# Four graph layers on one core: the expansions of the cell lists load the key rows of two groups with one transfer

## The reference, cut to what matters

```python
# layer 2: both directions of each edge
h = x @ W.T + b
msg = h[src] * norm
out = jax.ops.segment_sum(msg, dst, num_segments=num_nodes)
...
# layer 3: source rows alone are fetched
h_src = feat_n[src]
copy_sum = jax.ops.segment_sum(h_src, dst, num_segments=N)
...
# layer 4: both directions, attention with a softmax over the edges of a node
logits = jax.nn.leaky_relu(s_node[src] + d_node[dst] + e_all, NEG_SLOPE) / T
h_src = xt[src]
out = jax.ops.segment_sum(att[:, None] * h_src, dst, num_segments=num_nodes)
```

## Time and profile before

| what | value |
|---|---|
| device time, median of 3 runs | 18736.65 us (18729.88 to 18747.82) |
| profiled execution, span from first to last instruction | 18902.1 us |
| mean granted TensorE clock | 0.647 of full speed |
| busy over the span: PE, DVE, POOL, ACT | 60%, 54%, 48%, 24% |
| DMA issues of key rows by SP in the three expansions | 1632 of list 1, 1088 of list 0 |
| DMA issues of stores by SP in them | 1088 of 192 KB, 544 of 132 KB |

### The profile page before, as it was taken

The page is one execution under the profiler, slowest core; times in us unless marked ns, Lnnn a source line. Parts: engine busy times, 40 slices in busy tenths (PEclk is TensorE's granted clock), DMA queues, the critical chain, the costliest instruction groups (busy, mean ns, idle before and its releaser), DMA issues. The chain is left out here.

```text
span 18902.1 us, 333620 instructions
## 1 busy us (share of the span) xinstructions
PE 11316.2 (60%) x72558; PEld 8597.6 (45%) x72559; DVE 10279.5 (54%) x36111; ACT 4453.3 (24%) x11901; POOL 9045.6 (48%) x10035
## 2 busy tenths in 40 slices
PE   6555555555544666666586666655555665557886
PEld 5333333333333555555475444442223554336776
DVE  9555555555551333333564777773345554777776
ACT  0111111111110222222211342005400112555665
POOL 0555666555562555555674344540263344553332
PEclk9676677666665666666555566765555555557887
DMA  9522222222213222222433698766642777885454
GB/s 378 209 64 64 64 63 64 64 67 61 63 58 64 56 57 57 57 57 57 73 58 36 227 307 283 216 190 215 200 127 69 222 230 222 262 259 178 172 172 140
DMA packets 2144090, 2589.10 MB, mean 137 GB/s; under 512 B 892242, under 2 KB 1761563, under 8 KB 2143939
## 3 DMA queue, kind: packets, MB, share of 16 engines
q1 hardware_dynamic: 1748902, 1741.10, 31.4%
q0 software_dynamic: 353792, 654.90, 11.7%
q10 hardware_dynamic: 41244, 191.56, 2.6%
HBM read 1738.16 MB, written 848.30 MB: 137 GB/s over the span
## 5 line engine op out<-in xcount | busy, mean ns | idle before, releaser
L565 POOL DMA_INDIRECT edges_by_dst<-rec,pos x1568 | 1538.0, 981 | 2027.1 <-DVE rec L500 1577.6
L983 POOL DMA_INDIRECT sc_rows<-src_table,sc_idx x1664 | 1581.7, 951 | 1470.2 <-DVE sc_tp L1081 820.7
L565 POOL DMA_INDIRECT edges_by_cell<-rec,pos x1568 | 1549.2, 988 | 528.9 <-issue 527.4
L1719 PE MATMUL ex_rows<-table,ex_oh 128*128 x6528 | 1177.8, 349 | 830.4 <-DVE ex_oh L1687 406.7
L1805 PE MATMUL gs_part<-gs_rows,gs_oh 128*128 128x192 bf16 x6528 | 1093.2, 329 | 789.5 <-DVE gs_oh L1778 403.9
L1033 PE MATMUL sc_loc<-dst_table,sc_ohT 128*128 x3328 | 772.2, 405 | 1137.7 <-ACT sc_ohT L999 1090.8
L1767 POOL DMA_INDIRECT gs_rows<-rows_by_src,chunk_read_by_src x1088 | 1072.3, 986 | 759.5 <-PE gs_part L1805 441.2
L2213 PE MATMUL at_part<-cell_edge_term,key_in_block 128*66 128x128 f32 x8704 | 1229.6, 306 | 251.0 <-issue 211.5
L1719 PEld LDWEIGHTS ex_rows<-table,ex_oh 128*128 128x128 bf16 x6528 | 755.2, 132 | 1252.9 <-issue 1213.7
L2213 PEld LDWEIGHTS at_part<-cell_edge_term,key_in_block 128*66 128x66 f32 x8704 | 1143.0, 159 | 326.4 <-issue 314.8
L529 DVE SCALAR_TENSOR_TENSOR junk<-rowb,keycol,earlier 128x128 f32<-128x128 f32 (+1 forms) x3136 | 1150.7, 413 | 199.5 <-issue 195.3
(11 more groups left out here) (394 smaller groups left out, 25919.0 us busy)
## 6 DMA issues: line engine op xcount, KB each, us to landing
ex_keys<-src_key_rows SPq DMA_DIRECT2D x1632, 128.0 KB
rows_by_src<-ex_stage SPq DMA_DIRECT2D x1088, 192.0 KB
rowb<-sort_key_rows SPq DMA_DIRECT2D x392, 512.0 KB
ex_keys<-dst_key_rows SPq DMA_DIRECT2D x1088, 128.0 KB
dst_rows_by_src<-patY ACTq DMA_DIRECT2D x1, 104448.0 KB
gs_rows<-dst_rows_by_src SPq DMA_DIRECT2D x544, 192.0 KB
scored_dst_rows_by_src<-patZ ACTq DMA_DIRECT2D x1, 71808.0 KB
scored_rows_by_src<-ex_stage SPq DMA_DIRECT2D x544, 132.0 KB
```

Of the source, the lines that this page charges most:

```text
L565: nc.gpsimd.indirect_dma_start(out=out, out_offset=bass.IndirectOffsetOnAxis(ap=pos[:, u, k, j:j + 1], axis=0), in_=row, in_offset=None).t ...
L983: nc.gpsimd.indirect_dma_start(out=rows[:, u, j, :], out_offset=None, in_=tabS, in_offset=bass.IndirectOffsetOnAxis(ap=idx[:, u, j:j + 1], ...
L1719: m = nc.tensor.matmul(rows[k][u % 2][r // 2][:, r % 2, 0:W], oh[k][:, u % 2, r * P:(r + 1) * P], t3[:, bass.ds(held[k][u], 1), :].rearran ...
```

## The change

A load moves the keys of two groups, 2048 bytes into each partition, and is issued at even steps only. Its wait asks for one more group's one-hots than before, since it writes two slots. There is one key semaphore for each pair of slots. The bytes that are moved, the ring of four slots, and the work of all other engines are the same. The edit is the same in `expand_rows` and in `attention_rows`; one of them stands here.

```diff
-def row_of(kr, g):
+def row_of(kr, g, count=1):
 
     at = kr[0:1, 0:1]
-    return bass.AP(tensor=at.tensor, offset=at.offset + g * (SLOTS * P), ap=[[0, P], [1, SLOTS * P]])
+    return bass.AP(tensor=at.tensor, offset=at.offset + g * (SLOTS * P), ap=[[0, P], [1, count * SLOTS * P]])
...
-        s_key = {k: [counts.get(f"expand_keys_loaded{k}{u}") for u in range(RING)] for k, _, _ in lists}
+        s_key = {k: [counts.get(f"expand_keys_loaded{k}{u}") for u in range(RING // 2)] for k, _, _ in lists}
...
                 def load(i, u):
+                    if u % 2:
+                        return
                     g = i * RING + u
                     for k, kr, _ in lists:
-                        wait(sp, s_oh[k], g - RING + 1)
+                        wait(sp, s_oh[k], g - RING + 2)
                         sp.nop(nofuse=True)
-                        sp.dma_start(keys[k][:, u, :], row_of(kr, g)).then_inc(s_key[k][u].sem, 16)
+                        sp.dma_start(keys[k][:, u:u + 2, :].rearrange("p g e -> p (g e)"), row_of(kr, g, 2)).then_inc(s_key[k][u // 2].sem, 16)
...
-                        wait(dve, s_key[k][u], (i + 1) * 16)
+                        wait(dve, s_key[k][u // 2], (i + 1) * 16)
```

More of the change, by code:

```diff
@@ L1826, in attention_rows @@
         rows = [[ctx.enter_context(nc.psum_tensor(f"{name}_rows{k}{u}", [P, SLOTS, W], F32)) for u in range(2)] for k in range(2)]
-        s_key = [[counts.get(f"expand_keys_loaded{k}{u}") for u in range(RING)] for k in range(2)]
+        s_key = [[counts.get(f"expand_keys_loaded{k}{u}") for u in range(RING // 2)] for k in range(2)]
         s_oh = [counts.get(f"expand_onehots{k}") for k in range(2)]
```

## The result

The change took 18842.67 us (median of 9 runs, 18767.44 to 18857.25) against 18747.82 of the kernel before (9 runs beside it): ratio 1.0044, 95% interval 1.0033 to 1.0056. I had predicted 18410, with 0.85 for faster; it lies outside the range of 18160 to 18640 and on the other side of no change.

The account below looks back on a forecast made before the run. The prediction took SP's instruction stream to bound all three stages. Gains of 71, 46 and 210 us in ex1, ex2 and ex3, together 327, came off 18736.65 us to give 18410, with a range of 18160 to 18640.

Parts of the forecast that it names:

- The sum: Whole kernel: gains of 71 us in ex1, 46 in ex2 and 210 in ex3, together 327 us.
- SP's stream: All three stages: SP's instructions bound them; halved loads free 0.62 us a group in ex1 and ex3, 0.33 in ex2.
- The DMA engines: Ex1's next bound: about 1.87 us of DMA work a group, running at 2.0 with a share of 0.94.
- a saving of 0.1 to 0.15: Ex1: DMA time saved per group, in us, by fewer, larger pieces, from 2.00 us of work.
- The landing: Time from a key load's issue to its one-hot, slightly longer for pairs: 0.2 us in ex2, 0.3 in ex1.
- my formula: Period is landing plus one-hots and SP's reaction, over three groups in ex1 (1.90 us), four in ex2 (1.26).
- One more key load's engine time at most: Upper limit on how much later a doubled transfer lands: 0.5 us; 0.2 was taken for ex2.
- held up at other places for 0.4 a group: Ex3: SP's steps make 1.92 us of the 2.316 period; the unexplained rest was counted as SP's.
- My ring formula: Ex3: three periods must hold the key landing and about 0.7 us, (4.4 + 0.5 + 0.7) / 3 = 1.87 us.
- The slower rival: All stages: shorter lead and landing 1.5 us later cost 147 us, giving 18885 us; chance 0.08.
- The signs that I named: Changed trace: 272 loads of 0.34 us, longer SP waits, ex1 DMA share above 0.9, PE over three quarters busy in ex3.
- three signs of a wrong argument: SP waits for nothing at an unchanged period, ex2 falls to 1.03 us, or a pair's DMA instruction lasts near 0.7.

Follow-up runs that it names:

- v0: The kernel before, unchanged, traced again on one chip as the reference: ex1 1158.2 us, ex2 737.6, ex3 1253.4.
- v1: The change, unchanged, run again on one chip beside the kernel before: 1.0019 of its time.
- y4: Kernel before, with list 1's stores issued by ACT one step behind its eviction instead of by SP: 0.9999.
- z4: Against the kernel before: ex1 and ex3 with single loads and list 1's stores issued by ACT, ex2 with pairs in a ring of eight: 0.9936.
- z2: Kernel before, with a ring of eight key slots and single transfers eight groups ahead: 0.9961.
- z3: Pairs in a ring of eight, list 0's loaded at even steps and list 1's at odd ones, against the kernel before: 0.9898.
- x4: The change's pairs in all three stages, with a ring of eight and loads eight groups ahead, against the kernel before: 1.0000.
- v3: Pairs in a ring of eight, the two lists' loads at different steps, timed on another chip against the kernel before: 0.9886.
- v2: The change with list 1's pairs loaded at odd steps, ring of four kept: 1.0026 of the kernel before.
- y3: The change, with each partition reading at a place of its own, so with wrong keys: 0.9868 of the kernel before.
- y1: The change's waits and steps, but each pair loaded by two single transfers of 1024-byte pieces: 1.0108 of the kernel before.
- x1: The change's pairs in ex1 alone, against the kernel before: 1.0070, or +107 us.
- y2: Kernel before, single loads, with each partition reading at a place of its own, so with wrong keys: 0.9981.
- x2: The change's pairs in ex2 alone, against the kernel before: 0.9987, or -19 us.

## Why the prediction was wrong, by its steps

The sum had 71 us of gain in ex1, 46 in ex2 and 210 in ex3. On one chip (v0, v1) it was a loss of 69, a gain of 8 and a gain of 25.

- **SP's stream.** The work removed was right: issues halved, each 0.355 us, and SP's waits went from 6 to 377 us in ex1. That its stream was the bound held in ex1 with another bound close behind: y4 relieved SP otherwise and gained 33 us there, z4 46 on a slower chip. With eight slots halved issues were worth 91 us in ex1 and 39 in ex2 (z2, z3).
- **The DMA engines.** The step "I take a saving of 0.1 to 0.15" failed: from 2.00 the work rose to 2.10 in v1. I had bounded it by "no saving"; it could also cost more. The rate "by bytes" (326 GB/s at full share) was that of staggered single transfers. Two pairs side by side made it 289 / 0.93 = 311.
- **The landing: the step that failed in ex1 and ex2.** The sum had 4.7 + 0.3 = 5.0 us for it in ex1 and 3.94 + 0.2 = 4.14 in ex2. From a load's issue to its first one-hot the medians over all loads went in ex1 from 5.3 (list 0) and 5.2 (list 1) to 6.1 and 6.6 us (v0, v1), in ex2 from 4.1 to 4.5. In ex1 two faults add up: I had read the last load of the stage, 4.7 us, where the median ones took 4.9 and 5.1 in that same trace, and the doubled load is used 0.8 to 1.4 us later, not 0.3. With 6.1 my formula gives ex1 (6.1 + 0.7) / 3 = 2.27, measured 2.259, and with 4.5 ex2 (4.5 + 0.7 + 0.2) / 4 = 1.35, measured 1.344. The formula comes out wherever SP issues as soon as a slot is free, so this alone doesn't prove the loop to be the bound. Shown it is by the ring of eight, which takes 45 us off ex1 and 46 off ex2 with the burst in place (x4) and 122 off ex1 without it (v3 against v2), and by y3. "One more key load's engine time at most" was the fault in ex1: there a pair stands behind another pair, and both land later; v2, which pulls them apart, gets 5.4 us.
- **Ex3: another step failed.** I had put its whole gain, the largest term, on SP's stream, and counted what the steps didn't explain ("held up at other places for 0.4 a group") as SP's. Relieved of a third of its issues SP gave ex3 3 to 8 us in y4 and 13 in z4, where the sum had 210. My ring formula gives 2.27 for v1's ex3, measured 2.262, but by chance: with eight slots it stays at 2.257 (v3). Nor is it keys that DVE waited for there:

```profile
DVE ex_oh L1880 <- PE ex_rows L1916: 349.5, 194, 2.5
DVE ex_oh L1880 <- remote: 181.4, 79, 4.4
DVE ex_oh L1880 <- DMA ex_keys<-dst_key_rows: 58.1, 47, 6.6
DVE ex_oh L1880 <- DMA ex_keys<-src_key_rows: 4.4, 6, 1.5
```

  These are v1's waits in ex3 ("remote": the profile names no one); the longest is for PE's products. What holds that loop at 2.26 us a group stays open. On the faster chip, where ex3 has a DMA share of 0.91, the landing does count: pairs cost it 51 us, and eight slots bring 33 of them back.
- **The slower rival** had the mechanism of ex1 and, for a landing 1.5 us later, 2.30 there; I gave it 0.08, since 512 KB land in 3.7 us. That row was no witness for a queue with a share of 0.94. Its 1.58 for ex2 didn't come.
- **The signs that I named.** Issues, the duration of one, SP's waits and ex1's DMA share came as said, and DVE's idle time for keys in ex2 stayed, 537 us. PE is busy in ex3 for 807 of 1234 us, not over three quarters. None of the three signs of a wrong argument showed: they looked at SP, and the error lay behind it.
- **The rule on issuing engines.** The Trainium skill (DMA: Bandwidth & Descriptors, Issuing engines are not separate DMA queues) has the time to initiate a DMA as usually small beside the DMA. y4 agrees over the whole program, 0.9999 with the stores' issues on another engine; z2 against z3 doesn't, with 133 us for SP's halved loads. The Trainium skill (Perfetto Trace Analysis, DMA Optimizations) also says that splitting into smaller chunks may let some start sooner. y1 split every pair in two and ex1 took 1223.1 us for x1's 1219.9: no gain here, with a DMA share of 0.92 and four slots.

Left open: why reads of one row land later was not tried further than y2 and y3. Why ex3 takes 2.31 us a group on some chips and 1.91 on another has no answer either; from one issue of SP to the next there, one step in twenty is over 1.5 us in v0 and over 0.94 us in x1, and the granted clock is 0.58 against 0.68, but neither is shown to be the cause. Pairs in turn with the ring of eight weren't timed on the faster chip.

## What to carry to other kernels

A ring counts its transfers, not its slots: a pair in a ring of four is a ring of two, and its refill waits for the second of two readers. Here merging paid only together with a deeper ring and with the merged loads of the two lists pulled apart, which turned +0.2 to +0.4% into -1.1%. An engine that never waits may be the bound by a hair: look at the next one's share (here 0.94) before pricing its relief, and don't book to it the time that no row explains. And a formula that reproduces the period isn't yet its cause: change the ring and look again.

## What the runs showed of the hardware

Loads of one HBM row into 128 partitions have a long tail. In ex1 1024-byte pieces took 46 ns in the median and 60 in the mean; 2048-byte pieces took 84 in the median, and in the mean 136 to 139 with two loads side by side (128 in x4, with eight slots), 123 staggered (v2), 114 staggered in a ring of eight (v3). The tail isn't that of the one row alone: with places of their own the mean was 110 ns in ex1 (y3) but 129 in ex2, where one row gave 119 (x2). What such places did shorten is the time from issue to one-hot, in ex2 from 4.1 to 3.0 us for singles and from 4.5 to 4.0 for pairs.

A load with 128 pieces holds SP for 0.34 us with 1024 bytes a piece and 0.355 with 2048. The kernel before took 16.2 ms on one chip and 18.7 to 18.9 on others, and the change's effect on ex3 has another sign there (+51 us, -25 us).
